# Attention heads with the division and the queries' low parts on another engine, queries projected in one pair, and idle products: one change to a two-layer transformer kernel

## The reference

```
x = x + attention0(layernorm(x), context)        # one head of width 128
x = x + ffn0(layernorm(x))                       # 8 experts, the best one per token
x = x + attention1(layernorm(x), context)        # 8 heads of width 64
x = x + ffn1(layernorm(x))                       # 32 experts, 4 per token, and a shared one

def attention1(x, context):                      # per head of 8
    q, k, v = x @ Wq, context @ Wk, context @ Wv
    attn = softmax(q @ k.T / 8)
    return concat(attn @ v) @ Wo + bo
```

## Time and profile before

| | us |
|---|---|
| Runs shown | 1430.83, 1428.16, 1428.94 |
| Median of the runs | 1428.94 |
| The profiled execution's own time | 1430.34 |
| Its span, first to last instruction | 1428.5 |
| TensorE busy | 1371.8 (96%) |
| VectorE busy | 1103.8 (77%) |
| GpSimd busy | 944.2 (66%) |
| ScalarE busy | 798.7 (56%) |

### The profile page before, as it was taken

One profiled execution on the slowest core, in us unless ns is written; L12 is line 12 of the kernel. 1 busy time (PEld: TensorE's weight loads), 2 busy tenths in 40 slices (PEclk: granted clock), 3 DMA queues, 4 the chain that ended last, 5 costly groups with the idle time before them and its releaser, 6 DMA issues.

```text
span 1428.5 us, 19977 instructions
## 1 busy us (share of the span) xinstructions
PE 1371.8 (96%) x6225; PEld 784.4 (55%) x6225; DVE 1103.8 (77%) x1439; ACT 798.7 (56%) x1587; POOL 944.2 (66%) x543
## 2 busy tenths in 40 slices
PE   5999998787999999999999999999999999999998
PEld 3877776533555455555554554555555455556665
DVE  8976666598878788777788878778887886776555
ACT  3458887323565665556565665555565565553432
POOL 5001112342889889898988988798888999986110
PEclk9999999966999999999999999999999999999999
DMA  6640000400000200200020020002002000000011
GB/s 173 205 128 16 18 18 9 93 4 0 1 1 1 51 8 1 50 9 0 1 57 1 1 50 8 1 1 58 1 1 47 8 1 1 8 1 24 19 42 38
DMA packets 80536, 41.37 MB, mean 29 GB/s; under 512 B 64301, under 2 KB 72254, under 8 KB 80166
## 3 DMA queue, kind: packets, MB, share of 16 engines
q1 hardware_dynamic: 80454, 40.28, 11.3%
HBM read 26.53 MB, written 13.74 MB: 28 GB/s over the span
## 4 chain that ended last, share of the span: by engine, by line
PE 84%; DVE 9%; DMA 4%; ACT 2%; issue 1%; SPq 0%; POOL 0%; DVEq 0%; ACTq 0%; POOLq 0%
PE ps L1479 24%; PE ps L1466 14%; PE ps L1467 12%; PE ps L1429 9%; DVE chunk_max L999 4%; DMA v_scratch<-v_stage 3%; PE ps L1416 3%; PE ps L1642 2%; PE ps L1287 2%; PE ps L1285 2%; PE ps L1286 2%; PE ps L1296 2%; PE ps L1297 2%; PE ps L1298 2%; PE ps L1629 1%; PE ps L1628 1%
## 5 line engine op out<-in xcount | busy, mean ns | idle before, releaser
L565 POOL TENSOR_TENSOR psums<-psums,probs 126x1024 f32<-126x1024 f32 (+1 forms) x392 | 823.2, 2100 | 110.7 <-ACT probs L756 61.7
L756 ACT ACTIVATE probs<-ps 126x512 f32<-126x512 f32 (+1 forms) x816 | 415.2, 620 | 282.8 <-PE ps L1467 263.3
L999 DVE TENSOR_REDUCE chunk_max<-ps 128x2 f32<-128x1008 f32 (+1 forms) x416 | 472.3, 1180 | 87.6 <-PE ps L1429 86.3
L1479 PE MATMUL ps<-probs,v_mem 126*64 126x512 f32 (+1 forms) x1632 | 389.8, 598 | 0.0
L1466 PE MATMUL ps<-q_heads,ring 128*126 128x512 f32 (+1 forms) x816 | 340.7, 418 | 0.9
L1467 PE MATMUL ps<-q_low,ring 128*126 128x512 f32 (+1 forms) x816 | 322.0, 395 | 0.0
L1065 DVE TENSOR_TENSOR xn<-xn,probs 126x512 f32<-126x512 f32 x126 | 236.1, 1873 | 24.2 <-ACT probs L756 19.4
L1479 PEld LDWEIGHTS ps<-probs,v_mem 126*64 126x64 f32 (+1 forms) x1632 | 111.6, 136 | 169.3 <-issue 118.5
L1466 PEld LDWEIGHTS ps<-q_heads,ring 128*126 128x126 f32 (+1 forms) x816 | 151.9, 186 | 86.8 <-issue 45.3
L717 ACT CAST ring<-ps 64x252 fp32r<-64x252 f32 (+1 forms) x356 | 128.3, 360 | 125.8 <-PE ps L1416 122.7
L1429 PE MATMUL ps<-ring,q_heads 64*128 64x504 f32 (+1 forms) x416 | 168.8, 475 | 19.0 <-DVE chunk_max L999 13.9
(11 more groups left out here) (218 smaller groups left out, 1409.4 us busy)
## 6 DMA issues: line engine op xcount, KB each, us to landing
v_scratch<-v_stage SPq DMA_DIRECT2D x51, 252.0 KB
v_mem<-v_scratch SPq DMA_DIRECT2D x8, 1606.5 KB
ctx_mem<-in_ctx_t SPq DMA_DIRECT2D x3, 803.2 KB, 9.2
vslot<-in_ctx_rows SPq DMA_DIRECT2D x51, 47.2 KB
pair_w<-in_f_pairs SPq DMA_DIRECT2D x17, 128.0 KB, 2.1
xn<-rden_scratch SPq DMA_DIRECT2D x14, 128.0 KB
pair_w<-in_f_pairs SPq DMA_DIRECT2D x17, 65.0 KB, 1.8
x_tok<-in_x SPq DMA_DIRECT2D x1, 512.0 KB, 4.3
```

What stands on the lines that cost most here:

```text
L565: pool.tensor_tensor(sums[0:r, 0:width], sums[0:r, 0:width], probs[0:r, n % PROBS, 0:width], ALU.add).then_inc(c_sum, 1)
L756: act.activation(probs[0:r, n % PROBS, cols(half)], ps[0:r, score_bank(t, half), :], ACT.Exp, scale=float(HD) ** -0.5).then_inc(c_exped, 1)
L999: dve.tensor_reduce(chunk_max[:, h % 2, i:i + 2, c], ps[:, banks[0]:banks[1] + 1, 0:group_tiles(c) * KT], AX, ALU.max).then_inc(c_reduced, 1)
L1479: ins = pe.matmul(ps[half * HD:(half + 1) * HD, B_ACC, :], v_tiles[0:r, h % 2, t, :], probs[0:r, n % PROBS, cols(half)], start=(t == 0), s ...
```

## The change

1. GpSimd gets `normalize(h - 1)` before its addition of tile 18 in head h; VectorE loses it.
2. The queries of head h+2 are projected in block 5 of head h (`QUERIES_AT`), after the first tile's values: both halves at once, each 64 columns wide, into the two partition halves of bank 1 (`q_proj_parts`). ScalarE copies the bank to the free half of `spread_sums` (`queries_out`, end of block 5), rounds from there into `q_heads` (end of block 6) and into `q_low` (end of block 7) (`queries_hi`). GpSimd takes the low parts out of SBUF (`queries_lo`) before its additions of tiles 32 and 40. TensorE's first second-half score of block 6 waits for the copy of bank 1; its waits for the low part of queries amid blocks 5 and 6 go.
3. `row_shift(h + 1)` moves from behind the second tile's scores of the last block to behind the first half of the third tile's.
4. Idle products (of the identity by itself, into banks that are free): one after each of the first pass's last six steps, five after it, three behind head 0's shift, three before the second coarse step of head 0.
5. After the last head TensorE projects heads 4, 5 and 6 first, then sums head 7's rows, then projects head 7 in two parts into two pairs of banks (`project_last`, `LAST_OUT`). VectorE adds the three heads' outputs first, then takes the reciprocals and adds head 7's output, two steps per pair of columns.

`c_spread` becomes `c_kept` and counts the copies of sums and of queries. Queries of heads 0 and 1 are projected as before.

```diff
+B_QUERIES, QUERIES_AT = 1, 5
+LAST_OUT = ((3, 4), (1, 7))
+def sums_kept(h):
+    return min(2 * h + 2, 2 * HEADS - 3)
+def queries_kept(h):
+    return 2 * h - 3
...
@@ GpSimd
+            def normalize(h):
+                pool.wait_ge(c_turn, 80 * h + 80)
+                pool.wait_ge(c_acc, h + 1)
+                pool.tensor_tensor(acc[:, h % BATCH, :], acc[:, h % BATCH, :], spread_sums[:, h % 2, :],
+                                  ALU.mult).then_inc(c_rden, 1)
+            def queries_lo(h, half):
+                raw = spread_sums[half * HD:(half + 1) * HD, (h + 1) % 2, :]
+                pool.wait_ge(c_kept, queries_kept(h))
+                if half == 0:
+                    pool.wait_ge(c_qhi, 2 * h + 2)
+                    hi = q_heads[0:HD, h % 3, cols(half)]
+                else:
+                    pool.wait_ge(c_qlow, h + 1)
+                    hi = q_low[HD:P, h % 3, cols(half)]
+                pool.tensor_tensor(q_heads[HD:P, h % 3, cols(half)], raw, f32(hi), ALU.subtract).then_inc(c_qlo, 1)
...
+                    if t == 4 * GT + 2 and h:
+                        pool.wait_ge(c_sum, adds_to(h, t - 1))
+                        normalize(h - 1)
+                        pool.wait_ge(c_rden, 2 * h)
+                    if t in (8 * GT, 10 * GT) and h + 2 < HEADS:
+                        half = (t // GT - 8) // 2
+                        pool.wait_ge(c_sum, adds_to(h, t - 1))
+                        queries_lo(h + 2, half)
+                        pool.wait_ge(c_qlo, 2 * (h + 2) + half + 1)
@@ ScalarE
+            def queries_out(h):
+                act.wait_ge(c_qproj, 2 * h + 2)
+                if h >= 3:
+                    act.wait_ge(c_rden, 2 * (h - 2))
+                act.copy(spread_sums[:, (h + 1) % 2, :], ps[:, B_QUERIES, :]).then_inc(c_kept, 1)
+            def queries_hi(h, low):
+                act.wait_ge(c_kept, queries_kept(h))
+                for half in range(2):
+                    dst = q_low[HD:P, h % 3, cols(half)] if low else q_heads[0:HD, h % 3, cols(half)]
+                    ins = act.copy(dst, spread_sums[half * HD:(half + 1) * HD, (h + 1) % 2, :])
...
-                        if t % GT == 2 and b in (5, 6) and h + 2 < HEADS:
-                            q_hi(h + 2, b - 5, B_AUX)
...
-                    if b == 7 and h + 2 < HEADS:
-                        q_rows(h + 2)
+                    if b == QUERIES_AT and h + 2 < HEADS:
+                        queries_out(h + 2)
+                    if b in (QUERIES_AT + 1, QUERIES_AT + 2) and h + 2 < HEADS:
+                        queries_hi(h + 2, b == QUERIES_AT + 2)
@@ VectorE
             def reciprocals(h):
+                if h:
+                    dve.wait_ge(c_rden, 2 * h)
...
-                    if b in (5, 6) and h + 2 < HEADS:
-                        q_lo(h + 2, b - 5, B_AUX)
...
-                    if b == 4 and h:
-                        normalize(h - 1)
...
+            add_outputs(1)
             reciprocals(HEADS - 1)
+            dve.wait_ge(c_x, 2)
             add_last_output()
-            dve.wait_ge(c_x, 2)
-            add_outputs(1)
@@ TensorE
+            def q_proj_parts(h):
+                pe.wait_ge(c_wq[h % 2], 16 * (h // 2 + 1))
+                for half in range(2):
+                    pe.matmul(ps[half * HD:(half + 1) * HD, B_QUERIES, :], wq1[:, h % 2, 0:HD], xn_t[:, cols(half)],
+                              start=True, stop=True).then_inc(c_qproj, 1)
...
+                if t == (QUERIES_AT + 1) * GT and k == B_QUERIES and h + 2 < HEADS:
+                    pe.wait_ge(c_kept, queries_kept(h + 2))
...
+                if step >= GROUPS_H * STEPS - 6:
+                    pe.wait_ge(c_kfull, AHEAD)
+                    idle(1, FIRST_KP)
+            idle(5, FIRST_KP)
             pe.wait_ge(c_qlo, 4)
             pe.wait_ge(ring_rows, 2 * AHEAD + 1)
             row_shift(0, B_AUX)
-            pe.wait_ge(c_kfull, AHEAD)
+            idle(3, FIRST_KP)
...
                         if k and h == 0 and b == 0:
+                            idle(3, B_KEYS)
                             pe.wait_ge(c_shift, 2)
...
                             scores1(h, t, half, reduced - len(before) // 2)
-                        if b == GROUPS_H - 1 and t % GT == 1 and h + 1 < HEADS:
-                            pe.wait_ge(c_exped, 2 * (TILES * h + b * GT) + B_SHIFT + 1)
-                            row_shift(h + 1, B_SHIFT)
+                            if b == GROUPS_H - 1 and t % GT == 2 and half == 0 and h + 1 < HEADS:
+                                pe.wait_ge(c_exped, 2 * (TILES * h + b * GT) + B_SHIFT + 1)
+                                row_shift(h + 1, B_SHIFT)
...
-                            if b in (5, 6) and h + 2 < HEADS:
-                                q_proj(h + 2, b - 5, B_AUX)
...
-                        elif b in (5, 6) and h + 2 < HEADS:
-                            pe.wait_ge(c_qlo, 2 * (h + 2) + b - 4)
...
+                            if b == QUERIES_AT and h + 2 < HEADS:
+                                q_proj_parts(h + 2)
...
-            project_out(BATCH, PAIRS[1], True, False)
+            for h in range(BATCH, HEADS - 1):
+                ins = project_out(h, PAIRS[1], h == BATCH, h == HEADS - 2)
+            ins.then_inc(c_out, 1)
+            sum_rows(HEADS - 1)
             pe.wait_ge(c_acc, HEADS)
-            project_out(HEADS - 1, PAIRS[0], True, True).then_inc(c_out, 1)
-            sum_rows(HEADS - 1)
-            project_out(BATCH + 1, PAIRS[1], False, False)
-            project_out(BATCH + 2, PAIRS[1], False, True).then_inc(c_out, 1)
+            project_last()
```

More of the change, by code:

```diff
@@ L729, in sums_out @@
                 act.wait_ge(c_sums, h + 1)
-                act.copy(spread_sums[:, h % 2, :], ps[:, B_SUMS[h], :]).then_inc(c_spread, 1)
+                act.copy(spread_sums[:, h % 2, :], ps[:, B_SUMS[h], :]).then_inc(c_kept, 1)
+            def queries_out(h):
[8 more added lines that the diff above has]
+                    ins = act.copy(dst, spread_sums[half * HD:(half + 1) * HD, (h + 1) % 2, :])
+                    if not low:
+                        ins.then_inc(c_qhi, 1)
+                if low:
+                    ins.then_inc(c_qlow, 1)
             for half in range(2):
@@ L1040, in add_last_output @@
             def add_last_output():
-                dve.wait_ge(c_out, 2)
                 dve.wait_ge(c_rden, 2 * HEADS - 1)
                 for t in range(TT):
-                    half, u = divmod(t, TT // 2)
-                    ins = dve.scalar_tensor_tensor(out=x_tok[:, t, :], in0=ps[:, PAIRS[0][half], tile_cols(u)],
+                    u, half = divmod(t, 2)
+                    t = half * (TT // 2) + u
+                    dve.wait_ge(c_out, 3 + u // 2)
+                    ins = dve.scalar_tensor_tensor(out=x_tok[:, t, :], in0=ps[:, LAST_OUT[u // 2][half], tile_cols(u)],
                                                    scalar=rden[:, t:t + 1], in1=x_tok[:, t, :], op0=ALU.mult, op1=ALU.add)
@@ L1482, in attend1, with project_last @@
                 ins.then_inc(c_attended, 1)
+            def project_last():
+                for u in range(TT // 2):
+                    for half in range(2):
+                        rows = slice(half * HD, (half + 1) * HD)
+                        ins = pe.matmul(ps[:, LAST_OUT[u // 2][half], tile_cols(u)], acc[rows, (HEADS - 1) % BATCH, tile_cols(u)],
+                                        wo1[rows, HEADS - 1, :], start=True, stop=True)
+                    if u % 2:
+                        ins.then_inc(c_out, 1)
             def sum_rows(h):
@@ L1602, in warm @@
                               start=True, stop=True)
-            warm(11, 1)
+            warm(11, 2)
             for t in range(TT):
```

22 lines of the change are left out of this document (8 added, 14 removed).

## The result

The changed kernel takes **1414.25 us** (median of four runs, 1411.16 to 1415.86) against 1428.55 for the kernel before on the same chip: a ratio of 0.989, 95% interval 0.9873 to 0.9908. Forecast were 1411.4 us and a range of 1405 to 1422. Time and sign are right; the working has two terms with the wrong sign, and their errors largely cancel. The profiled execution took 1413.19 us (span 1411.4), 17.1 less than the profiled one of before; the medians differ by 14.3. One execution of all, in the set of e4, took 5597.7 us at a granted clock of 1.000; its cause is not known, and it moves that median by 0.04 us.

What follows compares the result with a forecast made beforehand. TensorE was taken to bound the heads, made late by VectorE in blocks 4 to 7. Terms -18.8 - 1.4 - 0.1 + 3.0 - 0.2 = -17.5 took 1428.94 to 1411.4 us, range 1405 to 1422.

Steps and rivals of the forecast that it cites:

- two terms with the wrong sign: The moved shift at head boundaries, forecast +3.0 us, and the idle products around the first pass, forecast -1.4 us.
- What bounds the kernel: In the eight heads TensorE is nearly always busy; VectorE, late with the maxima in blocks 4 to 7, makes it wait.
- Part 1, size: Blocks 4 to 7 of the heads: moving multiplication and queries' low parts off VectorE saves 18.8 us.
- Part 1, cause: Blocks 4 to 6: VectorE's output multiplication (2.85 us) and queries' low parts with their wait make it late with the maxima.
- the bare price is not to be had: In the heads, beside an always adding GpSimd, VectorE's additions cost 1.88 us in the mean, not the undisturbed 0.69.
- GpSimd's ledger: In the heads GpSimd takes 4.1 us more work, lags 0.7 to 0.9 more per head, peaks near 6, costs nothing.
- Part 2: Head boundaries: the shift behind half a tile costs +0.5 us each, six times +3.0, bounds -2.6 and +9; last boundary -0.2.
- +0.37: Boundaries 0/1 to 5/6: VectorE's chain starts half a tile later, less 0.09 us of TensorE's wait.
- Part 3: First pass: idle products fill gaps and raise the clock before the scores, -1.4 us, bounds -2.2 and +1.0.
- Part 4: After the last head: the norm's steps start when half the last output is there, -0.1 us, bounds -0.5 and +0.3.
- The sum: Whole kernel: all terms together -17.5 us, from 1428.94 to 1411.4 us.
- Rival (a): VectorE's chain at the boundaries does not bind, so the shift gains 0.43 us six times: 1406 us, chance 0.10.

Runs made afterwards that it cites:

- e4: The changed kernel with each of GpSimd's 12 subtractions for the queries done twice: 1427.67 us, ratio 0.9988 to the kernel before.
- e3: The kernel before with only the multiplication of outputs moved from VectorE to GpSimd: 1424.76 us, ratio 0.9963.
- e6: The changed kernel with the multiplication of outputs back on VectorE at its old place in block 4: 1410.91 us, ratio 0.9868.
- e9: The kernel before with three unread GpSimd multiplications added ahead of tile 10 in heads 1, 3, 4, 5 and 6: 1423.01 us, ratio 0.9954.
- e5: The changed kernel with its idle products replaced by cheaper ones of 64 rows in the rounded format: 1410.82 us, ratio 0.9872.
- e7: The changed kernel run again with nothing changed: 1413.43 us, ratio 0.9879 to the kernel before.
- e1: The changed kernel without any of its idle products: 1411.16 us, ratio 0.9878 to the kernel before.

## Why the prediction was right or wrong

**What bounds the kernel**: right. TensorE sets the heads, VectorE made it late, and relieving VectorE brought the blocks to TensorE's length.

**Part 1, size**: right, forecast -18.8, measured -18.2 in blocks 4 to 7 (1.72, 3.27, 1.73, 3.32, 3.27, 3.29, 1.58 in heads 0 to 6). Blocks of 9.24 and 10.1, the copy of bank 1, ScalarE's copies and the prices of GpSimd's instructions (1.33, 1.50, 1.33 against 1.3, 1.2, 1.2) came out as worked.

**Part 1, cause**: incomplete. "The cause shows on VectorE. [...] In block 4 it also multiplies outputs" took the multiplication as what makes block 4 long. It needs two things: the multiplication, and an addition that meets a wide GpSimd add (2.72). Either alone leaves the block at 9.25: e3 took away the one, e6 and e9 the other. The rows to see it in were there: head 2 of the kernel before is 1.6 us shorter over these blocks, since its block 4 takes 9.23 with the same multiplication. GpSimd stood 0.63 us behind there, not 0.10, and the addition took 0.72. I booked head 2 at 1.8 instead of 3.4 and did not ask why it differed. The additions of blocks 2 to 5 there, 0.69 to 0.72, also speak against "the bare price is not to be had": it is had where GpSimd happens to be between two instructions, or nearly done with one.

**GpSimd's ledger**: no cost, as forecast, but from head 0 to 3 the lag grew by 0.7 us in all, not by 0.7 to 0.9 per head, and its peak is 4.8, not 6. Its wide adds became shorter (2426 ns against 2462), which fits that VectorE does less beside it; that was not tried by itself.

**Part 2**: the step that failed. Forecast +3.0 at the six boundaries and -0.2 at the last; measured -0.7 and 0.0. Chain and +0.37 at an unchanged addition are in line with the runs; the addition in it was mis-sized: 0.67 at three boundaries, 1.16, 1.18 and 1.35 at the other three, where it had been 1.55 to 1.59. Take what it got shorter at those three from 0.37, and -0.06, -0.01 and +0.17 are left, against -0.03, 0.00 and +0.21 measured. Where the chain doesn't bind the move gave 0.30, not the 0.43 worked out. I had taken an increase out of a range that reached both ways, though GpSimd's lag was forecast to move it.

**Part 3**: wrong sign, forecast -1.4, measured +1.1. The clock did rise before the scores, and the 1.4 for it came as 1.5. What failed is "the added products fill gaps": it put the idle products' own time at nothing, without a price. One takes 0.72 us where the gap is 0.33, and the six in a row at the end of the pass run to 343.19 and delay the shift; the way to the first score grew by 2.7 us. The upper bound of +1.0 was given for another reason (a clock that stays).

**Part 4**: forecast -0.1, measured 0.0; from the end of the values to the norm it is 7.74 us against 7.72.

**The sum**: -18.2 in blocks 4 to 7, -0.7 at the boundaries, +1.1 in the pass, that is -17.8 against a forecast of -17.5. That these agree is luck: Part 2 is off by 3.5 one way, Part 3 by 2.5 the other. The median moved 14.3 in one set of runs and, for the same program, 15.8 in the other. The time outside pass and heads moves by some microseconds, and the granted clock moves with it: ahead of the pass lie 277.2 us in e5's execution, where the clock stays up from 18 us on, and 284.1 in e7's, where it is back at the 1.2 GHz level from 25 to 35 us. That the clock makes the difference was not tried by itself. Rival (a), the chain that doesn't bind, is half true: it doesn't where the addition is short.

## What to carry to other kernels

Where VectorE and GpSimd both read pairs of SBUF tiles, as here, an instruction's price is set by when it meets the other's: look at the same instruction in a stage that runs well (here head 2) before naming a heavy neighbour as the cause, and try shifting one engine by a microsecond before moving work. Take the term that repeats in every loop from trace marks inside the loop; its differences are good to 0.2 us where totals are good to 2 or 3. A filler product has to be priced in the format and at the clock in which it will run, against the gap it is to fill.

## What the runs showed of the hardware

- A VectorE addition of 126x512 float32 with both inputs in SBUF took 0.67 to 2.77 us beside a busy GpSimd (the changed kernel). Whenever it took over 0.75, its end stood 0.55 us behind the end of the GpSimd instruction it met (72 of 72 in the kernel before). Where VectorE went first, GpSimd's 126x1024 addition took 3.32 us instead of 2.38.
- Three useless GpSimd instructions (1.35 us) in each of five heads made a kernel of 1430 us 0.46% faster (0.29 to 0.63).
- At the 1.2 GHz level an idle product of 128x128 float32 (two instructions) took 0.72 us between products in the rounded format and 0.48 in a run of its own kind.
- Products of 64 rows in the pass's gaps, with pauses of up to 0.34 us left, kept the granted clock at 0.50 until over 4 us after the scores began (e5), much as without any (3.9 us, e1); idle products of the full 128 rows had it rise 2 us before them.
